# Tiles 2 and 3 of the grouped convolution computed from shared half blocks and an edge term, in float32, with a reordered VectorE step

## The reference

```python
# x (128, 32, 512), conv weight (32, 8, 9), 4 groups, padding 4
c = conv1d(x, weight, groups=4) + (cond_128 @ c_weight.T)[:, :, None] + bias[None, :, None]
base   = c @ base_W.T + base_b                       # 512 -> 512
probs  = softmax(c @ router_W.T + router_b)          # 15 routes
topk_p, topk_i = top_k(probs, 8)
w      = sum of topk_p over the experts expert_map[topk_i]        # 8 experts
h      = c @ A.T                                     # 8 experts x rank 16
out    = x + base + ((h * w) @ B) * 2.0
```

## Time and profile before

| what | value |
|---|---|
| median of 3 runs | 184.52 us |
| the three runs | 184.43, 184.52, 621.96 us |
| the profiled execution | 184.44 us |
| its span, first to last instruction | 182.6 us |
| around the span | 1.84 us |
| busy in the span: PE, DVE, POOL, ACT | 178.4, 150.8, 139.8, 81.2 us |

### The profile page before, as it was taken

The page is one execution under the profiler, slowest core; times in us unless marked ns, Lnnn a source line. Parts: engine busy times, 40 slices in busy tenths (PEclk is TensorE's granted clock), DMA queues, the critical chain, the costliest instruction groups (busy, mean ns, idle before and its releaser), DMA issues.

```text
span 182.6 us, 3930 instructions
## 1 busy us (share of the span) xinstructions
PE 178.4 (98%) x1236; PEld 171.1 (94%) x1236; DVE 150.8 (83%) x509; ACT 81.2 (44%) x247; POOL 139.8 (77%) x139
## 2 busy tenths in 40 slices
PE   7999999999999999999999999999999999999993
PEld 3687999999999999999999999999999999999992
DVE  0597888898888889888888988889898889978673
ACT  3648743354544434454443445454344444422320
POOL 2118999999888898888889888888988887885620
PEclk9999999999999999999999999999999999999999
DMA  6999751757475553646565454656445721233304
GB/s 172 348 388 340 252 178 14 243 199 204 152 233 174 173 181 124 178 152 230 159 198 174 135 170 154 228 178 210 175 106 201 230 78 63 97 115 115 118 0 172
DMA packets 17876, 32.01 MB, mean 175 GB/s; under 512 B 1984, under 2 KB 3136, under 8 KB 17856
## 3 DMA queue, kind: packets, MB, share of 16 engines
q1 hardware_dynamic: 17424, 31.40, 53.1%
q10 hardware_dynamic: 432, 0.36, 0.6%
HBM read 23.36 MB, written 8.39 MB: 174 GB/s over the span
## 4 chain that ended last, share of the span: by engine, by line
PE 96%; DVE 2%; issue 0%; POOL 0%; DVEq 0%; POOLq 0%
PE wide_ps L606 62%; PE wide_ps L648 12%; PE conv_banks L592 11%; PE edge_bank L592 3%; PE conv_banks L606 2%; PE odd_bank L635 2%; PE wide_ps L554 2%; PE conv_banks L663 1%; PE conv_banks L565 1%; PE conv_banks L563 1%; DVE xr L966 1%; DVE y L856 0%; DVE y_rows L774 0%; PE edge_bank L621 0%; DVE y_hi L891 0%
## 5 line engine op out<-in xcount | busy, mean ns | idle before, releaser
L606 PE MATMUL wide_ps<-wide_hi,y_hi 128*128 128x400 f32 (+1 forms) x248 | 66.0, 326 | 0.1
L606 PE MATMUL wide_ps<-wide_hi,y_lo 128*128 128x400 f32 (+1 forms) x248 | 62.6, 313 | 0.0
L606 PE MATMUL wide_ps<-wide_lo,y_hi 128*128 128x400 f32 (+1 forms) x248 | 62.5, 313 | 0.0
L486 POOL TENSOR_TENSOR terms_lo<-terms,terms_hi 128x512 fp32r<-128x512 f32 x28 | 36.3, 1298 | 18.4 <-ACT terms_hi L385 18.4
L606 PEld LDWEIGHTS wide_ps<-wide_hi,y_hi 128*128 128x128 f32 x248 | 44.0, 188 | 2.5 <-issue 0.5
L606 PEld LDWEIGHTS wide_ps<-wide_lo,y_hi 128*128 128x128 f32 x248 | 45.9, 188 | 0.0
L606 PEld LDWEIGHTS wide_ps<-wide_hi,y_lo 128*128 128x128 f32 x248 | 45.9, 188 | 0.0
L504 POOL TENSOR_TENSOR y_lo<-y,y_hi 128x512 fp32r<-128x512 f32 x31 | 40.3, 1299 | 5.7 <-ACT y_hi L400 5.7
L481 POOL TENSOR_TENSOR xr<-xr,base_b_sb 128x512 f32<-128x512 f32 x32 | 41.7, 1302 | 0.0
L407 ACT ACTIVATE hw_hi<-odd_bank 128x128 fp32r<-128x128 f32 x31 | 8.6, 278 | 54.3 <-PE odd_bank L635 54.3
L768 DVE TENSOR_TENSOR xr<-wide_ps,xr 128x512 f32<-128x512 f32 x30 | 20.7, 691 | 5.2 <-PE wide_ps L648 3.8
(11 more groups left out here) (90 smaller groups left out, 308.4 us busy)
## 6 DMA issues: line engine op xcount, KB each, us to landing
xr<-x_rows SPq DMA_DIRECT2D x32, 256.0 KB, 3.6
out<-xr SPq DMA_DIRECT2D x31, 256.0 KB, 3.2
terms<-x_units SPq DMA_DIRECT2D x28, 256.0 KB, 2.9
edges<-x_edges SPq DMA_DIRECT2D x14, 256.0 KB, 3.1
wide_sb<-wide_w SPq DMA_DIRECT2D x4, 328.0 KB, 4.9
x_in<-x_first SPq DMA_DIRECT2D x3, 264.0 KB, 4.7
weights_sb<-conv_w SPq DMA_DIRECT2D x2, 192.0 KB, 5.3
x_in<-x_first SPq DMA_DIRECT2D x2, 132.0 KB, 2.8
```

Source lines behind the costliest of these rows:

```text
L486: nc.gpsimd.tensor_tensor(terms_lo[i % 2][:, :, :, :], terms[i][:, :, :, :], terms_hi[i % 2][:, :, :, :].bitcast(F32), ALU.subtract)\
L606: mm = nc.tensor.matmul(sums_of(t, k)[:, b, 0:columns[1] - columns[0]], a[k % 2][:, r, :], w[:, r, columns[0]:columns[1]], start=r == 0 an ...
```

## The change

Tiles 2 and 3 leave `conv_first` for a new `conv_whole`: one float32 product for the shared term, one for the difference, and for tile 2 one for the edge term of both tiles, 256 columns each. Their inputs arrive as `first_terms` and `first_edges` in place of `x_in`; POOL makes the difference of tile 2 and that of the edges, DVE that of tile 3. The convolution weights shrink from 14 to 12 blocks and come in another order. `wide_lo` of run 1 is made by POOL. On DVE the edge part of `condition` becomes `reach`, later in the step, and `turn(t+2)` moves from the front of the step to its end, for all tiles. On ACT `y_high(t+1)` goes behind `hw_high(t-1)`, except in step 30. On POOL `bias_rows(0)` goes ahead of `edge_low`.

```diff
-            load_x(2)
+            load_first_terms(0)
             sync.wait_ge(wide_in[0], 16)
+            sync.dma_start(first_edges[:, :, :, :], x_edges[0]).then_inc(first_edges_in, 16)
+            load_conv(4)
+            sync.wait_ge(wide_in[1], 16)
             load_conv(3)
-            load_x(3)
+            load_first_terms(1)
             sync.wait_ge(wide_in[2], 16)
...
-                if up_to_tile(t, TILES - 2):
+                if t == TILES - 2:
+
                     y_high(t + 1, k + 1)
                 if t == TILES - 1:
                     exponentials(t, k)
                 hw_high(t - 1, k - 1)
+                if up_to_tile(t, TILES - 3):
+                    y_high(t + 1, k + 1)
...
             conv_low(0)
+            pool.wait_ge(wide_hi_ready, 2)
+            wide_low_part(nc.gpsimd, 1, wide_lo_second)
+            pool.wait_ge(first_terms_in[0], 16)
+            nc.gpsimd.tensor_tensor(first_terms[0][:, 0, :, :], first_terms[0][:, 0, :, :],
+                                    first_terms[0][:, 1, :, :], ALU.subtract)\
+                .then_inc(first_difference[0], 1)
+            pool.wait_ge(first_edges_in, 16)
...
                     terms_low(t + 4, k)
                     up_low()
-                    edge_low(p + 2, k // 2)
                     pool.wait_ge(base_b_in, 16)
                     bias_rows(t, k)
+                    edge_low(p + 2, k // 2)
                     y_low(t + 2, k + 2)
...
-            def conv_later(t):
+            def conv_whole(t):
+
+                i, h = t - FIRST, t % 2
                 pe.wait_ge(y_rows_ready, t - 1)
-                pe.wait_ge(conv_w_in[2], 16)
-                pe.wait_ge(x_loaded[t], 16)
-                conv_first(t)
+                pe.wait_ge(conv_w_in[2 + i], 16)
+                pe.wait_ge(first_terms_in[i], 16)
+                nc.tensor.matmul(conv_ps[:, h, 0, :, :], conv_sb[:, W_SUM[t], :],
+                                 first_terms[i][:, 1, :, :], start=True, stop=True)
+                pe.wait_ge(first_difference[i], 1)
+                mm = nc.tensor.matmul(conv_ps[:, h, 1, :, :], conv_sb[:, W_OWN[t], :],
+                                      first_terms[i][:, 0, :, :], start=True, stop=True)
+                if h == 0:
+
+                    pe.wait_ge(cond_biased, GROUPS)
+                    pe.wait_ge(first_edge_ready, 1)
+                    mm = nc.tensor.matmul(edge_ps, conv_sb[:, W_QUARTERS[t // 2], :],
+                                          first_edges[:, 0, :, :], start=True, stop=True)
+                mm.then_inc(conv_done, 1)
...
-            for r in range(RUNS):
-                wide_low(r)
+
+            wide_low(0)
+            wide_low(2)
+            wide_low(3)
             dve.wait_ge(cond_biased, 2)
...
                 if up_to_tile(t, TILES - 3):
                     condition(t + 2, (k + 2) % GROUPS, q + (k + 2) // GROUPS)
-                    turn(t + 2, k + 2)
-                    hw_low(t - 1, k - 1)
-                elif t == TILES - 2:
+                if up_to_tile(t, TILES - 2):
                     hw_low(t - 1, k - 1)
...
-                if up_to_tile(t, TILES - 2):
-                    choose(t, k)
-                    dve.wait_ge(logits_ready, t + 1)
-                    if up_to_tile(t, TILES - 5):
-                        difference(t + 4, k)
-                    best(t, k)
-                    dve.wait_ge(top_ready, t + 1)
-                    if up_to_tile(t, TILES - 3):
-                        add_out(t - 1, (k - 1) % UNROLL)
-                    mark(t, k)
-                    weigh(t, k)
+                choose(t, k)
+                dve.wait_ge(logits_ready, t + 1)
+                best(t, k)
+                if up_to_tile(t, TILES - 3):
+                    reach(t + 2, (k + 2) % GROUPS)
+                    add_out(t - 1, (k - 1) % UNROLL)
+                dve.wait_ge(top_ready, t + 1)
+                mark(t, k)
+                if up_to_tile(t, TILES - 5):
+                    difference(t + 4, k)
+                weigh(t, k)
+                if up_to_tile(t, TILES - 3):
+                    turn(t + 2, k + 2)
```

More of the change, by code:

```diff
@@ L31 @@
 START = 4
+FIRST = 2
 FIRST_ROWS = (slice(0, Q // 2), slice(Q // 2, Q))
@@ L100, in build @@
         zero_exp = sb("zero_exp", [P, 1])
-        x_in = [sb(f"x_in{i}", [P, Q, BLKI]) for i in range(START)]
+        x_in = [sb(f"x_in{i}", [P, Q, BLKI]) for i in range(FIRST)]
+        first_terms = [sb(f"first_terms{i}", [P, 2, Q, MK]) for i in range(START - FIRST)]
+        first_edges = sb("first_edges", [P, 2, Q, MK])
         terms = [sb(f"terms{i}", [P, 2, Q, MK]) for i in range(URING)]
@@ L156, in build @@
         x_first_in = [sem(f"x_first_in{i}") for i in range(2)]
-        x_loaded = [sem(f"x_loaded{i}") for i in range(START)]
+        x_loaded = [sem(f"x_loaded{i}") for i in range(FIRST)]
+        first_terms_in = [sem(f"first_terms_in{i}") for i in range(START - FIRST)]
+        first_edges_in = sem("first_edges_in")
+        first_difference = [sem(f"first_difference{i}") for i in range(START - FIRST)]
+        first_edge_ready = sem("first_edge_ready")
         cond_summed = sem("cond_summed")
@@ L222, in up_to_tile, with wide_low_part @@
             return t <= most
+        def wide_low_part(ops, r, ready):
+            ops.tensor_tensor(wide_lo[:, r, :], wide_sb[:, r, :], wide_hi[:, r, :].bitcast(F32),
+                              ALU.subtract).then_inc(ready, 1)
         def sums_of(t, k):
@@ L416, in _ @@
             bias_condition(range(1, 2), 2)
+            bias_condition(range(2, GROUPS), 3)
             conv_high(1)
@@ L688, in first_step @@
                         linear(0, 0, (r,), products=(Y_REST,), last=(RUNS - 1, W_REST))
-                for r in runs[:RUNS // 2]:
-                    pe.wait_ge(wide_lo_ready, r + 1)
-                    linear(0, 0, (r,), products=(W_REST,))
+                pe.wait_ge(wide_lo_ready, 1)
+                linear(0, 0, (0,), products=(W_REST,))
+                pe.wait_ge(wide_lo_second, 1)
+                linear(0, 0, (1,), products=(W_REST,))
                 cond_sums(range(2, GROUPS), 2)
-                pe.wait_ge(wide_lo_ready, RUNS)
+                pe.wait_ge(wide_lo_ready, RUNS - 1)
                 for bank, done in ((FRONT_BANK, front_done), (NEXT_BANK, linear_done)):
@@ L870, in wide_low @@
                 dve.wait_ge(wide_hi_ready, r + 1)
-                nc.vector.tensor_tensor(wide_lo[:, r, :], wide_sb[:, r, :],
-                                        wide_hi[:, r, :].bitcast(F32), ALU.subtract)\
-                    .then_inc(wide_lo_ready, 1)
+                wide_low_part(nc.vector, r, wide_lo_ready)
             def y_low(t, k):
@@ L909, in step @@
                 if t == 0:
-                    condition_first(2)
+                    condition(2, 2, 0)
+                    reach(2, 2)
                     turn(2, 2)
+                    hw_low(0, 0)
                     choose(1, 1)
@@ L914, in step @@
                     best(1, 1)
+                    condition(3, 3, 0)
+                    reach(3, 3)
+                    return
+                if t == 1:
+                    add_out(0, 0)
                     dve.wait_ge(top_ready, 2)
                     mark(1, 1)
-                    condition_first(3)
-                    hw_low(0, 0)
-                    return
-                if t == 1:
+                    difference(START + 1, 1)
+                    weigh(1, 1)
                     turn(3, 3)
-                    difference(START + 1, 1)
-                    add_out(0, 0)
-                    weigh(1, 1)
                     return
```

69 lines of the change are left out of this document (38 added, 31 removed).

## The result

| what | before | after |
|---|---|---|
| median | 184.83 us (6 runs) | 187.79 us (6 runs, 186.79 to 188.79) |
| the profiled execution | 184.44 us | 187.15 us |
| its span | 182.6 us | 185.3 us |

The 184.83 us count the run of 621.96 us in; the other five have a median of 184.58.

What follows compares the result with a forecast made beforehand. PE's own instructions were taken to bound the kernel. From the profiled 184.44 us, a head gain of 0.1 and an end wait of 1.6 gave 185.9 us; forecast 185.6 to 186.15 (chance 0.37), range 184.9 to 187.0.

Steps and rivals of the forecast that it cites:

- What comes off PE: PE's products of tiles 2 and 3: shorter by 0.40 and 0.84 us, together a gain of 1.24 us.
- Inputs: Loads of tiles 2 and 3: 4.3 us of cover for tile 3's larger load, so cost nothing.
- POOL in the prologue: PE waits 0.46 us for up_lo and 0.17 for edge_lo, leaving the head a gain of 0.6 if nothing collides.
- The overlap that no row shows: Prologue, POOL's wide_lo beside DVE's: between a head gain of 0.6 us and a loss of 0.4.
- the middle of two bounds: The value taken for the prologue overlap of POOL and DVE: a head gain of 0.1 us.
- the full price: Prologue: one engine waits for the whole of the other, head loses 0.4 us; as a rival 186.4 us, chance 0.26.
- DVE's step: Steps' new DVE order: 0.2 us of room stays in 5.32, no step grows, cost nothing.
- The end: Tile 31's front bank: PE waits 1.6 us for y_lo behind the late turn(31); tile 30's 0.4 lies inside.
- The sum: Whole kernel: 184.44 - 0.1 + 1.6 = 185.9 us.

Runs made afterwards that it cites:

- e7: The changed kernel with the old DVE and ACT order from step 2, wide_lo whole on DVE, POOL's differences waiting for it: 185.82 us, ratio 1.004.
- e8: The changed kernel, wide_lo whole on DVE, POOL's differences waiting for it, transposes directly behind hw_low in steps 28 and 29: 185.69 us, ratio 1.002.
- e12: The changed kernel, wide_lo whole on DVE, POOL's differences waiting for it, turn(31) ahead of add_out(28), y_high(30) ahead of hw_high(28): 185.45 us, ratio 1.003.
- e2: The changed kernel with run 1 of wide_lo given back to DVE: 186.99 us, ratio 1.013.
- e1: The changed kernel with tile 31 reached and turned ahead of hw_low in step 29, y_high(30) ahead of hw_high(28): 186.76 us, ratio 1.011.
- e6: The changed kernel with the old order of DVE and ACT from step 2 on: 187.78 us, ratio 1.012.
- e9: The kernel before plus one POOL difference of run 1's wide_lo operands into an unread spare buffer: 187.5 us, ratio 1.012, runs in two groups.
- e5: The kernel before with the new order of DVE, ACT and POOL in the steps: 186.86 us, ratio 1.010.
- e10: The kernel before plus four POOL memsets to spare tiles in the prologue, reading nothing: 184.88 us, ratio 1.003.
- e3: The changed kernel with the edits of e1 and e2 together: 185.53 us, ratio 1.003.
- e11: The changed kernel with POOL waiting for y_lo of tile 0 ahead of its wide_lo: 187.58 us, ratio 1.015.
- e4: The kernel before with run 1 of wide_lo made by POOL, the other three on DVE: 186.5 us, ratio 1.010.

## Why the prediction was wrong

- **What comes off PE: right.** The products of tiles 2 and 3 come every 0.43 us; five of them replace four of 0.86, 1.3 us less (1.24 was said). At `turn_hw(0)` 1.10 of it is left in the changed kernel.
- **Inputs: right.** PE waited for no load of tile 2 or 3.
- **POOL in the prologue: the waits right, the gain too high.** The waits for `up_lo` and `edge_lo` take 0.64 in the changed kernel (1.10 - 0.46) and 0.63 was said. But the head was to gain 0.6 if nothing collides, and no run shows that: it is 0.46 from tile 2 on where `wide_lo` collides, and 0.21 to 0.27 in e7, e8 and e12. There POOL makes `y_low(1)` later, and its collision with the difference of tile 3 wasn't in this term.
- **The overlap that no row shows: this step failed.** It took the middle of two bounds, a gain of 0.1, and the price was the full one or more: POOL's `y_low(1)` is 1.10 late, where 0.95 was worked out for the full price. The head lost 0.62 in the profiled execution, the upper end of what was worked out for the full price. The middle stood for nothing that could happen: the engines exclude each other or they don't. The rows that spoke for free were of another kind, as the text itself said, and the full price stood as a rival at 0.26. That rival's 186.4 is low by 1.4 too, for want of the terms below. Two consequences weren't seen: POOL's two differences read two SBUF operands as well (e2, 0.5 us of e2's head), and POOL can get ahead of DVE's `y_lo` of tile 0, on which PE waits directly (e1, e6, e9).
- **DVE's step: right that it doesn't outgrow PE's, wrong that no step grows.** This term was put at nothing, and the steps added 0.5 us. The kernels with the new convolution show 21.28 us for four steps, the kernel before, e5 and e10 21.23, with no wait of PE in either; over 28 steps this is 0.3. It isn't tied to the convolution, since e9, without it, takes 21.32. No run tells what it is. Another 0.14 comes with the new order around t = 25: in every kernel that has it there (e1, e2, e3, e5, e8, e11, e12) `hw_high(24)` starts 0.65 behind `turn_hw(24)`, in no other one. Why ACT is late there stays open.
- **The end: right, link by link.** 1.6 was said and 1.60 measured, 1.49 by the start of PE's front bank and 0.11 by the slow first product behind the wait; the 0.43 of tile 30 (0.4 was said) lies inside it, as said.
- **The sum.** 185.9 + 0.7 (overlap) + 0.5 (steps) gives 187.1, the profiled execution (187.15). The median lies 0.6 higher. Of this, 0.1 to 0.4 is shared by the kernel before, whose median was 184.83 in the comparison (184.58 without the run of 621.96) and not 184.44. The rest would be executions in which POOL is ahead of `y_lo` or the first input is late. The two groups of e9 and the rows of e1 speak for the first; e11, which forbids it, brought 0.2 where 0.3 to 0.8 was expected. No slow execution of the changed kernel was profiled, so this is argued, not shown.

## What to carry to other kernels

Before work goes from one engine to an idle one, look where the operands of both lie, not how much room the idle engine has: in e4 0.75 us of work taken off DVE made the head 0.6 us longer instead of shorter, because both then read two operands from SBUF, and the whole time 1.8 us longer. When the unknown is whether two things exclude each other, price the two cases and take one; the middle is no case. A profile is one execution: before a shift is put down to an edit, look when the first input landed in it. When an instruction moves later in a loop, check its last turn by itself: in 27 steps the late `turn` cost nothing, in step 29 it cost 1.6 us, and moving that one back mended it.

## What the runs showed of the hardware

- DVE and POOL, each with two SBUF operands, lengthen each other in the records instead of waiting: `wide_lo` on DVE 0.77 to 1.43 each, `y_lo` 0.69 to 1.96, DVE's difference of tile 3 0.42 to 1.07, POOL's differences 0.74 to 1.33. The view of waits shows none of it, only a longer instruction, and PE's wait for its end.
- POOL writing alone (2.42 us of `memset`) lengthened no row of DVE in the profiled execution of e10; four other executions of it were some 1.8 us slower and stay unexplained.
- The wait of PE at 175.17 cost 0.27 us more than the idle time that is listed for it (0.16 ahead of it, 0.11 behind), and the profile counts that as busy. A hold with 0.1 us of idle time or less isn't listed at all (`up(24)`; `up(2)` in e4).
- The landing of the first input varies between executions: the first `y_rows` starts between 6.03 and 7.46 us in the profiled ones. A late one moves the whole program nearly one for one (e5: 0.95 and 0.94; e10: 0.16 and 0.22), an early one less (e8: 0.47 and 0.23). Which of two engines is first in a collision, and so its price, can depend on that.
- Two kernels have 0.35 us more around the span than the others (e4 and e6: 2.13 to 2.23 in each execution, the others 1.75 to 1.89). A comparison of spans alone would miss it. Its cause is open.
